# A six-layer block in fp32 on one core: the token shift moved from matmuls into copies and a DMA, a shorter root, and new orders of all queues

## The reference

```python
def shift_tokens(t):            # the right half of the features comes from the token before
    a, s = jnp.split(t, 2, -1)
    s = jnp.pad(s, ((0, 0), (1, 0), (0, 0)))[:, :-1]
    return jnp.concatenate([a, s], -1)
def attn_layer(x, Wqkv, qs, ksc, Wo):      # 16 heads of 64, windows of 32 tokens
    q, k, v = jnp.split(x @ Wqkv, 3, -1)
    q = l2norm(q) * qs;  k = l2norm(k) * ksc          # then rotary tables with a scale
    return local_attention(q, k, v) @ Wo
def ffn_layer(x, g, bln, W1, b1, W2, b2):
    a, gate = split((layernorm(x) * g + bln) @ W1 + b1, 2)      # halves of 341
    return a * gelu(gate) @ W2 + b2
for i in range(6):
    x = attn_layer(shift_tokens(x), ...) + x
    x = ffn_layer(shift_tokens(x), ...) + x
```

## Time and profile before

| | us |
|---|---|
| median of 3 runs (lowest to highest) | 1872.15 (1868.36 to 1875.66) |
| profiled execution, own time | 1868.75 |
| its span, first to last instruction | 1867.0 |
| mean granted TensorE clock | 0.983 of full speed |

### The profile page before, as it was taken

How to read it: one execution, slowest core, us unless ns; L and a number is a source line. 1 busy time by engine, 2 the same in 40 slices (tenths; PEclk the granted TensorE clock), 3 DMA queues, 4 the chain that set the end, 5 groups by cost and what they waited for, 6 DMA issues and landing times. The chain is left out here.

```text
span 1867.0 us, 66200 instructions
## 1 busy us (share of the span) xinstructions
PE 1732.8 (93%) x26984; PEld 1428.9 (77%) x26985; DVE 1472.2 (79%) x2952; ACT 1404.0 (75%) x2772; POOL 1479.4 (79%) x1830
## 2 busy tenths in 40 slices
PE   6999967899999999999999999999999999999985
PEld 4788755777778888787887787877778877888773
DVE  5878847778977888888879787888888798889752
ACT  3777744678877888878877877888788878788862
POOL 3777757779888887988888879789888888898860
PEclk9999988999999999999999999999999999999998
DMA  4000011111121111111110211112111101110100
GB/s 140 1 1 1 1 36 34 31 44 32 31 68 44 33 43 32 58 44 42 44 32 22 68 44 43 31 33 67 40 37 44 32 22 41 38 50 22 37 27 23
DMA packets 45485, 70.67 MB, mean 38 GB/s; under 512 B 15476, under 2 KB 28928, under 8 KB 45184
## 3 DMA queue, kind: packets, MB, share of 16 engines
q1 hardware_dynamic: 43712, 64.34, 11.8%
q10 hardware_dynamic: 1472, 2.10, 0.3%
HBM read 21.33 MB, written 1.05 MB: 12 GB/s over the span
## 5 line engine op out<-in xcount | busy, mean ns | idle before, releaser
L1087 POOL TENSOR_TENSOR ra<-ra,rb 128x512 f32<-128x512 f32 x384 | 492.3, 1288 | 116.7 <-DVE rb L1083 111.6
L1132 POOL TENSOR_TENSOR qn<-ra,rs 128x512 f32<-128x512 f32 x384 | 401.3, 1058 | 7.2 <-POOL rs L1125 0.8
L1062 DVE TENSOR_REDUCE ss<-sq 128x8 f32<-128x512 f32 x384 | 260.4, 678 | 91.2 <-ACT sq L1051 91.2
L1214 POOL TENSOR_TENSOR sp<-sp,rl 128x512 f32<-128x512 f32 x192 | 200.0, 1046 | 61.7 <-DVE rl L1209 61.0
L1201 ACT ACTIVATE sp<-sp 128x512 f32<-128x512 f32 x192 | 121.7, 634 | 38.5 <-DVE sp L1196 38.1
L1205 DVE TENSOR_REDUCE sm<-sp 128x8 f32<-128x512 f32 x192 | 128.6, 670 | 15.5 <-ACT sp L1201 13.0
L1179 PE MATMUL pP<-kT,qT 64*32 64x64 f32 x4608 | 106.9, 226 | 2.8 <-issue 2.2
L1179 PEld LDWEIGHTS pP<-kT,qT 64*32 64x32 f32 x4608 | 93.8, 105 | 16.3 <-ACT kT L1152 11.0
L489 POOL TENSOR_TENSOR ra<-ra,rb 128x512 f32<-128x512 f32 x64 | 81.5, 1288 | 29.6 <-DVE rb L485 29.6
L1190 DVE TENSOR_REDUCE mx<-pS 128x8 f32<-128x512 f32 x48 | 32.9, 685 | 91.2 <-PE pP L1179 91.2
L1083 DVE TENSOR_TENSOR rb<-pQ,rope 128x512 f32<-128x512 f32 x144 | 97.9, 680 | 2.9 <-POOL ra L1087 2.9
(11 more groups left out here) (355 smaller groups left out, 6194.3 us busy)
## 6 DMA issues: line engine op xcount, KB each, us to landing
vs<-v SPq DMA_DIRECT2D x96, 384.0 KB, 3.3
wqkvA<-in_L_ffn_Wqkv SPq DMA_DIRECT2D x18, 512.0 KB, 5.6
vs<-v SPq DMA_DIRECT2D x96, 64.0 KB, 3.0
woB<-in_L_ffn_Wo SPq DMA_DIRECT2D x6, 512.0 KB, 4.2
w<-in_L_ffn_W SPq DMA_DIRECT2D x6, 341.0 KB, 2.9
out<-x SPq DMA_DIRECT2D x4, 256.0 KB, 2.3
x<-in_L_attn_x SPq DMA_DIRECT2D x1, 768.0 KB, 8.1
w<-in_L_ffn_W SPq DMA_DIRECT2D x12, 64.0 KB
```

The lines of the kernel that those rows point to most:

```text
L1062: e.tensor_reduce(ss[:, j, :], sq[:, j % 2, :].rearrange("p (h d) -> p h d", d=DB), AX.X, ALU.add).then_inc(b_ss.sem, 1)
L1087: e.tensor_tensor(ra[:, j, :], ra[:, j, :], rb[:, j % 2, :], ALU.add).then_inc(b_ad.sem, 1)
L1132: e.tensor_tensor(qn[:, j % 4, :].rearrange("p (h d) -> p h d", d=DB), ra[:, j, :].rearrange("p (h d) -> p h d", d=DB), rs[:, c % 2, 8 * j ...
L1214: e.tensor_tensor(y, y, rl[:, u, :].unsqueeze(2).to_broadcast([P, 8, 64]), ALU.mult).then_inc(b_pn.sem, 1)
```

## The change

Five things change at once.

1. `xt_turn` transposes the two tiles whole, without a shift (two transposes in place of five matmuls). The shift is in where `xt_high` and `xt_low` write: the lower 64 partitions go to the same column, the upper 64 one column on. Each becomes two instructions. Column 0 of the upper half is set to zero once.
2. `l_shift` is no longer on PE. SP copies whole rows of `xr` one partition down into `fx` by one DMA and the right halves of the last partition's even tiles by a small one. `l_first` is on ACT, waits for both and writes the left halves. `l_second`, `SHIFT_BANK` and semaphore `f_sh` are gone.
3. The root has nine steps: steps 0 to 4 on POOL, 5 to 8 (a polynomial, each a scalar_tensor_tensor) on DVE.
4. Layer 0's output, norm and hidden weights are loaded before the stream, the next layer's projection weights after the moves of batch 3, and the `finish` of a pair runs on DVE in the pass that is two behind.
5. The lists of the four engines and of SP are new, and with them the banks of PSUM. Both `xt_turn` of a pair stand at its beginning now. More of the odd batch (turns 0 to 3, its first scores) is left to the next pass. Some waits are for certain passes alone.

The first attention and the barrier behind it are as before.

```diff
-NORM = 12
-ROOM = (1024.0 / 27.0) ** 2
+NORM, FIT = 9, 5
+SERIES = (1.0, -0.49999832, 0.37500061, -0.3139403, 0.27406215)
+ROOM = 1.0 / SERIES[4] ** 2
+HORNER = [x / SERIES[4] for x in SERIES[3::-1]]
...
         def xt_turn(e, l, c):
...
             for t in range(NT):
-                e.matmul(o[lo, t * P:(t + 1) * P], xc[:, t, lo], ident, start=True, stop=True)
-            e.matmul(o[hi, 0:P], xc[:, 0, hi], down, start=True, stop=True)
-            e.matmul(o[hi, P:T], xc[:, 1, hi], down, start=True, stop=False, skip_group_check=True)
-            e.matmul(o[hi, P:T], xc[:, 0, hi], wrap, start=False, stop=True, skip_group_check=True)\
-             .then_inc(b_xt.sem, 1)
+                i = flip(e, o, t, xr[:, (c % B) * NT + t, :])
+            i.then_inc(b_xt.sem, 1)
+
+        def shifted(l, c, x_):
+
+            o = xt_bank(l, c)
+            return ((x_[0:HALF, c % 2, :], o[0:HALF, 0:T]), (x_[HALF:M, c % 2, 1:T], o[HALF:M, 0:T - 1]))
...
-            e.copy(xsh[:, c % 2, :], banks[XT_BANK[c % 2]][:, 0:T]).then_inc(b_xh.sem, 1)
+            for dst, o in shifted(l, c, xsh):
+                i = e.copy(dst, o)
+            i.then_inc(b_xh.sem, 1)
...
-            e.tensor_tensor(xsl[:, c % 2, :], banks[XT_BANK[c % 2]][:, 0:T], xsh[:, c % 2, :].bitcast(F32),
-                            ALU.subtract).then_inc(b_xs.sem, 1)
+            for (dst, o), (h, _) in zip(shifted(l, c, xsl), shifted(l, c, xsh)):
+                i = e.tensor_tensor(dst, o, h.bitcast(F32), ALU.subtract)
+            i.then_inc(b_xs.sem, 1)
...
             elif n == 4:
-                e.tensor_scalar(p, t, -10.0 / 3.0, None, ALU.add).then_inc(b_rs.sem, 1)
...
+                e.tensor_scalar(t, t, -1.0, None, ALU.add).then_inc(b_rs.sem, 1)
+            elif n == FIT:
+                e.scalar_tensor_tensor(p, t, HORNER[0], t, ALU.add, ALU.mult).then_inc(b_rs.sem, 1)
+            elif n < NORM - 1:
+                e.scalar_tensor_tensor(p, p, HORNER[n - FIT], t, ALU.add, ALU.mult).then_inc(b_rs.sem, 1)
             else:
                 e.wait_ge(b_qn.sem, b_qn.at(it - 2, QK - 1))
-                e.tensor_tensor(rs[:, c % 2, :], t, y, ALU.mult).then_inc(b_rs.sem, 1)
+                e.scalar_tensor_tensor(rs[:, c % 2, :], p, HORNER[n - FIT], y, ALU.add, ALU.mult).then_inc(b_rs.sem, 1)
...
         def l_shift(e, l, q):
...
+            e.wait_ge(f_ln.sem, f_ln.at(it - 1))
+            e.sem_inc(e_hold.sem, 1)
+            k = (q % FP) * FT
+            e.dma_start(fx[0:1, 1::NT, HALF:M], xr[P - 1:P, k:k + FT:NT, HALF:M]).then_inc(f_xs.sem, 16)
+            e.dma_start(fx[1:P, :, :], xr[0:P - 1, k:k + FT, :]).then_inc(f_xs.sem, 16)
 
         def l_first(e, l, q):
             it = l * FP + q
             e.wait_ge(b_wx.sem, b_wx.at(l * B + 2 * q + 1))
...
-            e.tensor_copy(fx[:, :, 0:HALF], xr[:, tiles(q), 0:HALF]).then_inc(f_xa.sem, 1)
...
+            e.wait_ge(f_xs.sem, f_xs.at(it))
+            e.copy(fx[:, :, 0:HALF], xr[:, tiles(q), 0:HALF]).then_inc(f_xa.sem, 1)
...
+            for load in (load_out, load_norm, load_hidden, load_second):
+                load(e, 0)
...
+                move_values(e, l, 2, 1)
+                l_shift(e, l, 0)
+                if l > 0:
+                    load_second(e, l)
+                move_values(e, l, 3, 0)
+                move_values(e, l, 3, 1)
+                if l < DEPTH - 1:
+                    load_ahead(e, l + 1)
```

More of the change, by code:

```diff
@@ L1457, in pair_pe @@
             if on(p - 1):
-                e.wait_ge(b_ev.sem, b_ev.at(l * B + c - 1, 3))
-                turn_p(e, l, c - 1, 0)
-                e.wait_ge(b_oc.sem, b_oc.at(l * B + c - 2, 3))
+                scores(e, l, c - 1, 0)
+            if on(p):
+                e.wait_ge(b_ab.sem, b_ab.at(l * B + c, 0))
+            if on(p - 1) and not on(p) and not on(p):
+                e.wait_ge(b_oc.sem, b_oc.at(l * B + c - 2, 2))
+            if on(p - 1):
+                turn(e, l, c - 1, 5)
@@ new lines, in pair_pe @@
+            if on(p):
+                e.wait_ge(b_ab.sem, b_ab.at(l * B + c, 1))
+                proj(e, l, c, 4)
+            if on(p - 1):
+                e.wait_ge(b_tc.sem, b_tc.at(l * B + c - 1, 3))
+                turn(e, l, c - 1, 6)
+                e.wait_ge(b_tc.sem, b_tc.at(l * B + c - 1, 4))
+            if on(p - 2) and on(p - 3) and not on(p - 1) and not on(p - 1) and not on(p - 1) and not on(p - 1) and not on(p - 1) and not on(p - 1) and not on(p - 1):
+                e.wait_ge(f_G.sem, f_G.at(l * FP + p - 3, 2))
@@ L1562, in pair_pe @@
             if on(p):
-                e.wait_ge(b_tc.sem, b_tc.at(l * B + c, 1))
-                proj(e, l, c + 1, 3)
+                scores(e, l, c, 0)
+                e.wait_ge(b_ab.sem, b_ab.at(l * B + c + 1, 2))
+                turn(e, l, c, 4)
+            if on(p - 1):
+                e.wait_ge(b_oc.sem, b_oc.at(l * B + c - 1, 2))
+            if on(p) and not on(p - 1):
+                e.wait_ge(b_tc.sem, b_tc.at(l * B + c, 2))
+            if on(p):
+                proj(e, l, c + 1, 4)
+                e.wait_ge(b_ev.sem, b_ev.at(l * B + c, 2))
+                proj(e, l, c + 1, 5)
+                e.wait_ge(b_tc.sem, b_tc.at(l * B + c, 4))
+                proj(e, l, c + 1, 6)
@@ L1587, in pair_pe @@
+            if on(p - 1) and not on(p):
+                e.wait_ge(b_oc.sem, b_oc.at(l * B + c - 1, 3))
             if on(p - 1):
                 out_proj(e, l, c - 1, 0)
+            if on(p):
+                scores(e, l, c, 1)
+                e.wait_ge(b_tc.sem, b_tc.at(l * B + c, 6))
+                turn_p(e, l, c, 0)
+            if on(p - 1):
                 out_proj(e, l, c - 1, 1)
             if on(p):
-                e.wait_ge(b_ab.sem, b_ab.at(l * B + c + 1, 5))
-                turn(e, l, c, 6)
@@ L2099, in dve_program @@
             scaled_rope(e, 0)
-            stream(e, pair_dve)
-            remainder(e, pair_dve)
-            for q in range(FP):
-                finish(e, q)
+            stream(e, pair_dve, lambda p: leave(e, p - DONE))
+            remainder(e, pair_dve, lambda p: leave(e, p - DONE))
         def pool_program(e):
```

787 lines of the change are left out of this document (399 added, 388 removed).

## The result

The changed kernel takes 2039.64 us (median of 4 runs, 2037.59 to 2043.49); the kernel before took 1871.43 beside it (4 runs). The ratio is 1.09, 95% interval 1.0872 to 1.0927: 9% slower, where 1826 us was forecast.

A forecast was written before the change was run, and what follows sets the result against it. TensorE's queue, 97% covered in the layers, was taken as the bound. 1868.75 - 49.2 (TensorE) + 5 (xt chain) - 3.9 + 2 (ends) = 1822.7, as a median 1826 us, 2.5% faster; range 1780 to 1872.

The forecast's parts named there:

- The shift by DMA: `l_shift` on SP to ACT's `l_first`: landing takes 4.5 us against a distance of some 5 us; charged nothing.
- rival C: Landing of the shift some 3 us late stalls ACT and TensorE each pair: slower, 1898 us; chance 0.10.
- TensorE's queue priced in full: TensorE in the pairs: shorter `xt_turn` and no `l_shift` save 2.05 us a pair, 49.2 us, counted fully as time.
- the sum: Whole kernel: 1868.75 - 49.2 + 5 - 3.9 + 2 = 1822.7 us, as a median of runs 1826 us.
- The chain of xt: `xt_turn`, `xt_high`, `xt_low` ahead of the first projection: longer with split halves, charged 5 us, bound 14 us.
- ACT's 0.8 us: ACT, per pair: net 0.8 us more work on 51.4 busy, hidden under TensorE; uncovered it would be 19 us.
- The small steps on DVE at 0.33: DVE, root steps 5 to 8: eight a pair at 0.33 us, 2.6 us, covered; bounds 1.6 to 6.2 us.
- its sign of being wrong: DVE's small root steps: the forecast is wrong if they take over 0.5 us each.
- The loads: Projection loads mid-layer on SP: still before the last pair splits them; DMA engines busy 15%, charged nothing.
- The ends: Kernel's end: fewer final multiplies and adds save 3.9 us; work left to the drain costs 2 us, bounds 0 and 5.3.
- Rival D: Transposes in a row make TensorE's clock fall once each pair, 3.5 us each: 84 us more, about 1910; chance 0.04.
- Rival B: Gain eaten by the xt chain (14 us) and waiting at the root or landing (24 us): 1859 us; chance 0.16.

The follow-up runs named there:

- the version with 126 and 1 rows: The changed kernel with the shift's DMA of 127 rows cut into two transfers, 126 rows and 1 row: 1859.83 us, ratio 0.995 to the kernel before.
- the shorter turn: The kernel before, `xt_turn` as two transposes, cast and subtraction whole and unshifted: 1905.63 us; with eight tiny matmuls ahead of each turn, 1870.10 us.
- the other two pairs of runs: The kernel before with the new turn and split halves, or the DMA shift alone: 1943.54 and 1931.31 us; stream length given back by tiny matmuls, 1909.56 and 1891.90.
- the root alone: The kernel before with only the nine-step root (0 and 1 on DVE, 2 to 4 on POOL, 5 to 8 on DVE): 1875.37 us, ratio 1.0025.

## Why the prediction was wrong

**The shift by DMA: the step that failed.** "0.6 + 0.6 + 3.3 = 4.5 us", "I charge nothing". From the first issue to ACT's copy were 14.6 us in the pair shown. The price was read from a move of 96 rows, and one of 127 rows is another thing: its packets run one after another, 127 x 84 ns = 10.7 us at least. The rest of the step held: ACT, its copies of attention output and TensorE stand in that order, as rival C says (a chance of 0.10, priced for a landing 3 us late; it came about 10 late, at 7.7 us of waiting a pair). 24 x 7.7 = 185 us of waiting, 180 in the runs. The Trainium skill (DMA: Bandwidth & Descriptors, Why a DMA increments its semaphore by 16 and not by 1) gives the rule: the engines used are the largest number up to 16 that divides the slowest dimensions, 1 for 127. By that rule, the trace agrees: 8% of sixteen engines, and 1.3 us where 126 rows allow 14.

**TensorE's queue priced in full: the second step that failed**, hidden behind the first. The busy times came out as forecast: from the windows of the version with 126 and 1 rows, a pair of 63.3 us in that trace has TensorE at 59.8 (forecast 61.5 - 2.05 = 59.5), DVE at 55.6 (55.5), POOL at 50.3 (49.2). But time did not follow TensorE. In the old orders 0.74 us less a pair gave 0 of 18 us. In the new ones the pairs behind the first last 63.3 us against 63.5 in the two profiles, where 1.85 us less was forecast, and the kernel without its block gaps is some 25 to 28 us better than before (1825 against 1853, or 1850 by the 1868.83 us that the kernel before took beside it), where 46 were forecast. With the turn alone put back, 31 us of work cost 17. That "the longest wait of TensorE for another engine is 6.0 us" over 16 pairs was true and was read as proof of a bound; "the 97% holds gaps too short to see" was the better sentence. Work taken away from TensorE was worth nothing there, while work added counted almost in full, so its queue was close to the bound but not alone. What stands beside it in the old orders was not isolated.

**What the sum left out: the end of a block of instructions.** It is worth +16 us for the version with 126 and 1 rows (35 against 19), and the sum has no term for it. 1826 + 16 + (46 - 28) = 1860 is the measured time split in these parts, and no further test of them. It takes a gap to cost its own length. Where only positions changed that held closely for the kernel before (61 us for 60 us of gaps) and for the shorter turn (36 for 34), less so for the other two pairs of runs (34 for 23, 39 for 30). Each change of TensorE's list moves all later groups in their blocks: in the kernel before, its groups of scores begin at 1 to 13, 37 to 43, 128 to 142 and 166 to 172 of a block in the layers, and most stalls come where they begin at 192 to 255: 17 of the 20 over 0.5 us inside such groups in the run with the shorter turn.

**The chain of xt.** Charged at 5 us, bound 14. In the new orders the halves cost 3 us: right, as far as 3 us can be told. In the old orders 38, with 24 us left when the stream's length is given back (1910 - 1870 = 40, of which 16 are gaps at block ends). The charge holds for the new orders only, where both turns stand far ahead.

**Covered and charged at nothing.** ACT's 0.8 us: right, within the 3 us. The small steps on DVE at 0.33: four took 2.06 us together (1.29 for the first) in the pair shown, so 0.5 each there, just where the prediction set its sign of being wrong; over the layers the first takes 1.16 us and the three behind it 0.23; the root alone was 4 us slower, within its interval of no change. The loads: "still before the last pair splits them. I charge nothing: DMA engines are busy 15%" missed that TensorE's own instructions come as DMA packets too, and late when other packets are under way; their old place was 4 us better, if that is a difference.

**The ends.** Forecast -3.9 + 2. From the start of the last pair to the end are 135.9 us with 126 and 1 rows against 129.9 before, 6 more. From the start of the last `out_add` on 2.4 us are saved (31.6 against 34.0), where 3.9 were forecast. Ahead of it stand 8.4 us more, where 2 were charged with 5.3 as the bound: likely the odd batch's work that the new orders leave to the drain; which part of it was not isolated. The first pair is 4 us shorter (56.7 against 61.0), which was left out.

**Rival D** had a chance of 0.04 and put the falls down to transposes in a row. The version with 126 and 1 rows has the same five groups, and behind its first pair the clock fell four times until the drain, each time 2.2 to 4.0 us after TensorE began to stand at a block end. That speaks for the standing still and against the transposes. The 3.5 us by which the rival's pair from 1103.3 us was longer were read wrongly as the price of a fall: 2.45 of them are a gap at a block end at 1162.1, whose packet came 6.2 us late, and the fall came behind it at 1164.3.

**Rival B** said 1859, and the version with 126 and 1 rows took 1859.83. That is luck: its terms, 14 us for the chain and 24 us of waiting for the root or the landing, did not come; gaps at block ends, the drain and work that was worth less than its length stand in their place.

## What to carry to other kernels

Price a DMA by a row of its own shape: here 127 rows were another transfer than 96 or 126, and one line cost 180 us. When a stream of small instructions is tuned to the last per cent, part of its time is where the 256-instruction blocks end: before a difference of 1 to 4% is put down to an edit, shift the stream by a few dozen harmless instructions and see what moves. An engine that is 97% busy is not shown to set the time until taking work from it has shortened something; that adding work lengthens it is not the same test.

## What the runs showed of the hardware that was not expected

56 harmless instructions at one place made a kernel of 1871 us 61 us slower; 128 at the same place 14 us. Where TensorE stands over 0.8 us at the end of a block, it goes on 2.2 to 3.0 us after the start of a packet of 16,384 bytes (3.7 once in all runs), and this packet can start late while data are under way: 7.4 us after the block's entry in the version with 126 and 1 rows, and 6.7 us in one where only packets of 128 bytes were left. Bursts of 128 matmuls of one column, 3.2 us long, came with falls of the clock: 16 falls and 95 us from 530 to 1800 us, in a kernel that had one. What an instruction block waits for inside the DMA engines, and what bounds the old orders' 61.4 us pair, stays open.
